# Four-layer graph network on one core: other places for the edge copies, the value loads, the low parts and the flips of layer 0

## What is computed

```python
q = x1.reshape(n, 8, -1).transpose(1, 0, 2) * SCALE      # x1 is x
k = x2.reshape(n, 8, -1).transpose(1, 0, 2)
vv = v.reshape(n, 8, -1).transpose(1, 0, 2)
scores = jnp.einsum('hnd,hmd->hnm', q, k)
scores = jnp.where(adj > 0, scores, NEG_FILL)
attn = jax.nn.softmax(scores, axis=-1)
out = jnp.einsum('hnm,hmd->hnd', attn, vv)
```

## Time and profile before

| | |
|---|---|
| median of 3 runs | 784.59 us (783.59 to 786.24) |
| the profiled execution | 784.18 us, span 782.5 us |
| layer 0 | to about 357.5 us of the span |
| layer 1 | about 357.5 to 588 us |
| layers 2 and 3 | about 588 to 782.5 us |
| busy, share of the span | PE 93%, DVE 84%, ACT 70%, weight loads 58%, POOL 14% |

### The profile page before, as it was taken

How to read it: one execution, slowest core, us unless ns; L and a number is a source line. 1 busy time by engine, 2 the same in 40 slices (tenths; PEclk the granted TensorE clock), 3 DMA queues, 4 the chain that set the end, 5 groups by cost and what they waited for, 6 DMA issues and landing times. The chain is left out here.

```text
span 782.5 us, 22935 instructions
## 1 busy us (share of the span) xinstructions
PE 726.0 (93%) x9908; PEld 454.3 (58%) x9908; DVE 657.7 (84%) x1001; ACT 545.3 (70%) x588; POOL 112.1 (14%) x220
## 2 busy tenths in 40 slices
PE   4798999999999999998889999999966999999996
PEld 1232333333333333336679999999963577776885
DVE  4797999999999999977899999999985757664544
ACT  7898999999999998773699999999904411111000
POOL 1421100310000000004310000000002323321222
PEclk9999999999999999999999999999996999999999
DMA  9998635363545451003271111101005000000001
GB/s 344 247 240 203 173 95 137 89 142 96 136 96 136 98 109 22 2 15 111 53 271 56 57 56 55 41 21 57 3 2 216 1 1 1 2 1 0 28 28 54
DMA packets 42599, 68.39 MB, mean 87 GB/s; under 512 B 4032, under 2 KB 27200, under 8 KB 40832
## 3 DMA queue, kind: packets, MB, share of 16 engines
q1 hardware_dynamic: 32976, 60.08, 25.3%
q0 software_dynamic: 9520, 6.82, 5.2%
HBM read 52.60 MB, written 10.09 MB: 80 GB/s over the span
## 5 line engine op out<-in xcount | busy, mean ns | idle before, releaser
L624 ACT ACTIVATE ex<-scores_ps,joint_shift 128x1024 f32<-128x1024 f32 x256 | 266.7, 1121 | 18.0 <-PE scores_ps L454 17.9
L707 DVE TENSOR_TENSOR esum<-esum,ex 128x1024 f32<-128x1024 f32 x188 | 217.2, 1216 | 1.2 <-ACT ex L624 1.2
L451 PE MATMUL scores_ps<-qst,kst 64*64 64x512 f16 x2048 | 158.7, 385 | 9.0 <-ACT ex L624 9.0
L1480 ACT ACTIVATE steps<-a_all,big_b_head 128x2048 fp8e5<-128x2048 f32 x86 | 163.6, 1988 | 0.0
L1195 PE MATMUL banks<-fx,pos 128*128 128x132 f16 x2048 | 159.4, 221 | 3.9 <-DVE pos L1387 3.7
L470 PE MATMUL mixed_total_ps<-ex,v 128*32 128x512 f32 x1024 | 125.6, 609 | 1.8 <-DMA v<-in_v_dram 1.8
L1195 PEld LDWEIGHTS banks<-fx,pos 128*128 128x128 fp8e5 x2048 | 120.6, 97 | 4.6 <-DVE pos L1387 2.6
L451 PEld LDWEIGHTS scores_ps<-qst,kst 64*64 64x64 f16 x2048 | 48.4, 106 | 116.0 <-ACT ex L624 84.7
L1202 PE MATMUL banks<-fm,edge 128*128 128x66 f16 x2048 | 103.7, 193 | 0.0
L454 PE MATMUL scores_ps<-masks,negI 64*64 64x512 bf16 x1024 | 99.8, 379 | 0.0
L1202 PEld LDWEIGHTS banks<-fm,edge 128*128 128x128 fp8e5 x2048 | 86.1, 97 | 0.0
(11 more groups left out here) (222 smaller groups left out, 722.9 us busy)
## 6 DMA issues: line engine op xcount, KB each, us to landing
adj_raw<-in_adjT_dram SPq DMA_DIRECT2D x32, 512.0 KB, 4.5
qst<-pieces_dram SPq DMA_DIRECT2D x28, 256.0 KB, 5.1
a_all<-score_rows_dram SPq DMA_DIRECT2D x7, 1024.0 KB, 6.6
edge<-masks POOLq DMA_DIRECT2D x32, 128.0 KB, 4.7
edge_copy_dram<-edge SPq DMA_DIRECT2D x1, 4096.0 KB, 17.1
edge_second<-edge_copy_dram SPq DMA_DIRECT2D x1, 4096.0 KB, 12.7
pieces_dram<-high_low SPq DMA_DIRECT2D x14, 256.0 KB, 4.2
ex<-in_x2T_dram SPq DMA_DIRECT2D x2, 1024.0 KB, 8.1
```

Of the source, the lines that this page charges most:

```text
L451: nc.tensor.matmul((one, two)[x][at], keys[rows, x, :], qst[rows, it % 2, half, 2 * p + x, :], start=(half == 0), stop=False, skip_group_c ...
L624: nc.scalar.activation(ex[:, slot(s), 2 * p:2 * p + 2, at], scores_ps[:, u % SR, :].rearrange("p (x n) -> p x n", n=CW), ACT.Exp, bias=joi ...
L707: nc.vector.tensor_tensor(esum[:, heads, at], other, ex[:, slot(s), heads, at], ALU.add).then_inc(summed, 1)
L1480: nc.scalar.activation(steps[:, pair_of(h, k) % SLOTS, jt % GU, :], aall[:, e, :], ACT.Relu, bias=bigh[:, e, jt:jt + 1], scale=BIG, satura ...
```

## The change

Five things move; nothing is computed in another way.

1. **Start.** SP waits for the first load of `v` before it issues `load_x(2)` and `load_x(3)`. DVE makes the low parts of jobs 2 to 4 before the two squares.
2. **Values of group 1** are loaded like those of group 0: once whole rows, then four swapped transfers, in step 4 (after the exponentials of steps 0 to 3), not in step 2.
3. **Edge copies** go by `EDGE_AT`: piece `m` in step `m + 5` or the step after its conversion, if that is later, and each also waits for the exponentials up to that step.
4. **High parts** of jobs 11 to 15 are made in steps 16, 24, 32, 40 and 48, one step earlier; **low parts** stay in step 17 and so on, but ahead of that step's first addition. SP loads and stacks these jobs one step earlier. In each step SP first stores, then loads, then stacks, over all jobs.
5. **Flips**: all 16 behind DVE's last step of layer 0, none in layer 1.

```diff
-    SPLIT_AT = {2: 5, 3: 6, 5: 7, 7: 8, 8: 9, 9: 10, 17: 11, 25: 12, 33: 13, 41: 14, 49: 15}
+    SPLIT_AT = {2: 5, 3: 6, 5: 7, 7: 8, 8: 9, 9: 10, 16: 11, 24: 12, 32: 13, 40: 14, 48: 15}
+    LOW_AT = {s + (s >= 2 * JP): j for s, j in SPLIT_AT.items()}
...
+    EDGE_AT = [max(m + 5, CONVERT_AT.get((m, 1), 0) + 1) for m in range(CONVERTED)]
+    SECOND_V_AT = 4
...
+                sp.wait_ge(v_landed[0], 16)
                 load_x(2)
                 load_x(3)
...
-                    for j in range(3, len(JOBS)):
-                        if LOAD_AT.get(j) == s:
+                    for j in STORE_AT:
+                        if STORE_AT[j] == s:
+                            store_pieces(j)
+                    for j in LOAD_AT:
+                        if LOAD_AT[j] == s:
                             load_natural(j)
-                        if STORE_AT.get(j) == s:
-                            store_pieces(j)
+                    for j in STACK_AT:
                         if STACK_AT[j] == s:
                             stack(j)
...
+                def load_v(g):
+                    pool.dma_start(vt[:, g], tiles(v)[:, :, g * GW:(g + 1) * GW]).then_inc(v_landed[g], 16)
+                    pool.wait_ge(v_landed[g], 16)
                     for h in range(1, HG, 2):
-                        load_swapped(0, h)
...
+                        load_swapped(g, h)
...
+                    if s == SECOND_V_AT:
+                        pool.wait_ge(exp_ready, s * UNITS)
+                        load_v(1)
+                    for m in range(CONVERTED):
+                        if EDGE_AT[m] == s:
+                            if s <= STEPS:
+                                pool.wait_ge(exp_ready, s * UNITS)
+                            keep_edges(m)
...
                 keep_shift(0)
-                make_low(2)
-                square(0)
-                for j in range(3, FIRST):
+                for j in range(2, FIRST):
                     make_low(j)
-                square(1)
+                for i in range(2):
+                    square(i)
...
+                        if i == 0 and s > 2 * JP and s in LOW_AT:
+                            make_low(LOW_AT[s])
...
-                        if i == 1 and s in SPLIT_AT:
-                            make_low(SPLIT_AT[s])
+                        if i == 1 and s < 2 * JP and s in LOW_AT:
+                            make_low(LOW_AT[s])
...
-                        if it in (3, 5, 7) and jp == 0:
-                            flip((it - 3) // 2, i)
+                for c in range(NC):
+                    for part in range(JP // 2):
+                        flip(c, part)
```

More of the change, by code:

```diff
@@ L138, in free_after @@
         return JP * (round_of(c, g) - 1) - 1 if what == "q" and c else -1
-    STORE_AT = {j: STEP_OF[j] + 1 for j in STEP_OF}
+    STORE_AT = {j: s + 1 for s, j in LOW_AT.items()}
     STACK_AT = {j: max(STEP_OF[j], free_after(j)) + 2 for j in STEP_OF}
@@ L350, in load_swapped @@
                         pool.dma_start(vt[to, g, :, at], of_v[of]).then_inc(v_landed[g], 16)
-                def load_first_v():
-                    pool.dma_start(vt[:, 0], tiles(v)[:, :, 0:GW]).then_inc(v_landed[0], 16)
-                    pool.wait_ge(v_landed[0], 16)
+                def load_v(g):
+                    pool.dma_start(vt[:, g], tiles(v)[:, :, g * GW:(g + 1) * GW]).then_inc(v_landed[g], 16)
+                    pool.wait_ge(v_landed[g], 16)
                     for h in range(1, HG, 2):
-                        load_swapped(0, h)
[L358 to L364, removed]
+                        load_swapped(g, h)
                 def keep_edges(m):
@@ L379, in _ @@
                 pool.wait_ge(xs_landed[1], 16)
-                load_first_v()
-                for m in range(AHEAD):
-                    keep_edges(m)
+                load_v(0)
                 for s in range(STEPS + 8):
[L384 to L389, removed]
+                    if s == SECOND_V_AT:
[6 more added lines that the diff above has]
+                            keep_edges(m)
                     if s == RANGE_AT + 2:
@@ L465, in mix @@
                     if s % JP == 0 and it < G:
-                        pe.wait_ge(v_landed[it], 16 * (1 + HG, 3 * HG // 2)[it])
+                        pe.wait_ge(v_landed[it], 16 * (1 + HG))
                     for t in range(2):
@@ L1049, in layer1 @@
             S.sem(n) for n in ("pos_ready", "unit_done", "half_done", "rest_step", "cut", "pieces_joined", "post_step"))
-        left_a, cut_a, negated, counted, fine_made, heads_made, flipped = (
-            S.sem(n) for n in ("left_first_a", "cut_first_a", "negated_first", "fine_counted", "fine_made", "heads_made",
-                               "marks_flipped"))
+        left_a, cut_a, negated, counted, fine_made, heads_made = (
+            S.sem(n) for n in ("left_first_a", "cut_first_a", "negated_first", "fine_counted", "fine_made", "heads_made"))
         a_landed = [S.sem(f"a_landed{e}") for e in range(2)]
@@ L1121, in body @@
                     if h == 0:
-                        sp.wait_ge(flipped, T // TG)
                         sp.dma_start(edge_copy, edge[:]).then_inc(edge_moved, 16)
@@ L1158, in _ @@
                 pe.wait_ge(normed, T - 1)
-                pe.wait_ge(flipped, T // TG)
                 degree.count(pe, ps[:, 1, :], range(T // 2 - 3))
@@ L1238, in largest @@
                                             ).then_inc(most_made, 1)
-                def flip(part):
-                    tt = slice(part * TG, (part + 1) * TG)
-                    marks = edge[:, tt, N - CW:N].bitcast(int32)
-                    nc.vector.tensor_scalar(marks, marks, BITS, BITS, ALU.bitwise_and, ALU.bitwise_xor).then_inc(flipped, 1)
                 nc.vector.memset(wh1[:, :, :, DH:DH + 1], TOP)
@@ L1250, in _ @@
                         measure(t)
-                    if t % TG == 2 and t < T:
-                        flip(t // TG)
                     if t % TG == 0 and t >= 2 * TG:
```

## The result

The changed kernel is slower: 789.32 us median (787.58 to 790.76, 7 runs) against 784.65 us (783.25 to 786.65, 7 runs) of the kernel before beside it, a ratio of 1.0057 (95% interval 1.0042 to 1.0072), so about 4.5 us. That is outside the forecast's range. The profiled execution is the slowest of the seven, 790.76 us with a span of 789.0 us, against 784.18 and 782.5 before.

The account below looks back on a forecast made before the run. Layer 0 was taken as bound by ACT with DMA nearly full to about 72 us, then PE, ACT and DVE, then PE in round 7. Terms +0.6 - 1.4 + 0.1 - 0.3 = -1.0 us gave 783.6 against 784.59, range 780.1 to 787.2.

Parts of the forecast that it names:

- The start: Layer 0 up to unit 3 of step 1: `v` early, adjacency piece 2 late, unit at 34.8 not 30.99, +3.8 us.
- the second halves then land near 24.0: Start: x's second halves, issued after `v` lands near 16.4, land 4.9 + 2.7 us later.
- the 1.8 us added to it for the swapped transfers: Start: q0's DMA time for `v`'s swapped transfers, 2.75 less 0.98 us for an edge copy; piece 2 lands about 27.0.
- the slow start of q0: Start: first packets of `v` of group 0 run about 4.8 us after its issue at 8.40.
- the bound of 28.5: Start: latest landing of piece 2, if a landing follows its last packet by another 1.5 us.
- Steps 2 to 8: Layer 0 after the start: ACT's waits of 1.80, 0.51 and 0.93 us go, -3.24 us, between nothing and -3.24.
- About even: Steps 2 to 8: DMA price of group 1's values as whole rows, 2.7 + 1.8 us against about 4.
- The third rival: Start and steps 2 to 8: DMA backlog not made up before step 6, +5.0 not +0.6 us, 788.0 us; chance 0.10.
- Rounds 2 to 7: Layer 0 round starts: low parts and flips gain, exposed high parts cost 0.52 us each; -1.4 us, between -0.8 and -3.2.
- Rival 2: Rounds: high part stays hidden in ACT's slack ahead of unit 3; rounds -3.2, whole -2.8, 781.8 us; chance 0.14.
- Flips at the end: End of layer 0: 16 flips take 5.4 us in a wait of 5.48 us; +0.1, between 0 and +1.3.
- Layer 1: Layer 1: four flips go, the last ahead of the last tile's statistics; -0.3 us, between 0 and -1.2.

Follow-up runs that it names:

- experiment 6: Changed kernel without SP's wait for `v` in the start and with `v` of group 1 issued in step 2, not 4: 780.07 us, ratio 0.9945.
- experiment 12: Changed kernel, its wait for `v` kept, with `v` of group 1 issued in step 2 instead of step 4: 787.88 us, ratio 1.0031.
- experiment 9: Kernel of experiment 6 with high parts of rounds 2 to 6 moved to the round's second step, behind the third exponential: 782.53 us, ratio 0.9980.
- experiment 8: Kernel before with only the flips at the end of layer 0 and the high and low parts moved: 781.95 us, ratio 0.9971.
- experiment 10: Kernel of experiment 6 with PE making the scores of unit 3 of step 1 ahead of the first mix: 779.30 us, ratio 0.9932.
- Experiment 5: Changed kernel, wait for `v` kept, with adjacency pieces 2 and 3 issued ahead of x's second halves: 789.67 us, ratio 1.0062.
- experiment 11: Changed kernel with SP's wait for `v` between `load_x(2)` and `load_x(3)` instead of ahead of both: 787.06 us, ratio 1.0030.
- experiment 2: Kernel before with only SP's wait for `v` added ahead of `load_x(2)` and `load_x(3)`: 793.58 us, ratio 1.0099.

## Why the prediction was wrong

**The start: the sign was right, the size was not.** The chain was as forecast: `v` early, piece 2 late, unit 3 of step 1 late with it. The wait itself was priced too low, at 3.8 us for 6.58. The step that failed is "the second halves then land near 24.0" and the 1.8 us added to it for the swapped transfers. That took q0's share of the engines for the whole price. Its share was as reckoned (31.3% of the 6 us from 20 to 26, 1.9 us), but q1 also got less done in what it had: the last half was there at 27.02, though `v` had landed 0.8 us earlier than assumed. The forecast also had the slow start of q0 for `v` alone. It came again for the swapped transfers, whose first packets ran 4.6 us and more behind their issue at 15.88, where it had been 2.0 to 2.5 us in the kernel before; nearly all of their 0.52 MB then ran from 20 to 26 us, beside the last half. What they would have cost it had they started sooner, no run shows. Piece 2 was then there at 29.31 instead of 27.0, just above the bound of 28.5, and from there to unit 3 it was 8.26 us, not 7.8.

**Steps 2 to 8: this step failed in kind.** "About even" for the values of group 1 counted the bytes in both shapes, and not when they run. The two waits of 1.80 and 0.93 us went, as forecast, and a new one of 2.68 us came, from values issued 4 us ahead of an adjacency piece. With that one edit put elsewhere the term was right: in experiment 6 the kernel is 1.77 us behind the kernel before at unit 3 of step 1 (32.76) and 1.58 us ahead at `total` of round 2 (111.95 against 113.53), -3.35 us, where -3.24 and +0.26 had been forecast. Which share of it the edge copies have, and which SP's order, no run shows. (The values of group 1 are six transfers in the kernel before, not eight; the bytes are as counted.)

**The third rival** ("the backlog stays", 788.0 us, 10%) came nearest in time: it had +5.0 us up to the rounds, and +5.79 was measured. Its mechanism was half right. The DMA time lost while SP waits is real and is in the 6.58 us. But experiment 12 shows no wait left of it from step 2 on; what stood in step 6 had another cause. The chance was too small, because I held against it only that the edge copies leave the stretch, and not that a megabyte of values moves into it.

**Rounds 2 to 7: right.** `total` of round 7 was to gain 1.4 us on the rounds' start and gained 1.80. By round the forecast had +0.26, -0.40, -0.83, -0.90 and -0.64 at rounds 2 to 6; from 5.79 us behind, the traces have +0.18 (119.50 against 113.53), -0.56 (158.80 against 153.57), -1.03 (198.14 against 193.38), -1.18 (237.44 against 232.83) and -0.99 (276.74 against 271.94). PE's wait for ACT was to be 0.88 us and is 0.86. Rival 2 is out, and experiment 9 shows why the trade is good.

**Flips at the end: right** as to the cover. 16 took 5.45 us, in the wait of 5.48 us of the earlier trace rows, and the first `transpose` follows at once. From `total` of round 7 to it are 37.14 us in the kernel before, and the same in experiments 6, 8 and 10, which have the flips there. The +1.65 us of this stretch come from round 7, and not from the flips: see below.

**Layer 1: not resolved.** The forecast had -0.3 us, the traces have +0.63, with a DMA of `bias` 3.89 us from issue to the instruction that waited for it before (363.11 to 367.00), and 4.86 us after (368.82 to 373.68). From that first `transpose` to `negb` the kernels without flips in layer 1 took between 31.4 and 33.6 us; so the stretch varies by more than the term.

## What to carry to other kernels

A wait ahead of a load prices the whole queue behind it, and lets the DMA engines idle until it ends; before adding one, ask which engine in-order work would have waited anyway, and whether a change in that engine's order (experiment 10) gets the same for nothing. When a transfer is moved or reshaped, look for the next urgent transfer issued within its own landing time in any queue, not only at the bytes. Where a gain could come from either of two engines at a barrier, try the one with the longer path.

## What the runs showed of the hardware that I had not expected

- **The software queue's slow start goes with the second halves.** I read 4.8 us from the issue of `v` to its first packets as a property of the software path. In the changed kernel it is issued at the same time, without the halves in q1, and q0 has packets in the stretch of 10 to 11 us, all of them behind 10.5, so 2.1 to 2.6 us behind the issue:

```profile
q1 hardware_dynamic: 133, 0.24, 68.2%
q0 software_dynamic: 13, 0.05, 54.1%
```

  The same stretch of the kernel before shows q1 alone. `v` landed 7.2 us after its issue instead of 10.8. It is not load as such: the swapped transfers of the kernel before began 2.0 to 2.5 us behind their issue with q1 at a share of 1, in packets of about 1.9 KB (1.28 MB in 679 packets, 19 to 23 us). With the halves in q1, in packets of 8 KB (0.81 MB in 102), it is 4.6 us and more in both kernels: for `v` in the one before, for the swapped transfers in the changed one. Experiment 5, whose swapped transfers are issued at 16.34 with the adjacency pieces ahead of the halves, has their first packets at 18.5 to 19. Whether it is the size of the packets or something else about the halves was not tested. The 1 us that the Trainium skill gives for it ("DMA: Bandwidth & Descriptors", Specifications), weighed in the prediction, is nearer to the shorter of the two than my reading was, though it isn't reached here either.

- **Round 7 has two lengths.** From its `total` to the first `transpose` of the end it is 37.14 us in six of the fourteen traces, those of the kernel before and of experiments 5, 6, 8, 10 and 11. It is 38.7 to 39.9 us in the other eight, the changed kernel's among them. PE has idled 2.45 to 3.25 us ahead of it in all. In the 15 us around this `total` the granted clock is 1.00 in the six short ones, 0.89 in seven of the long ones and 0.77 in experiment 2; two rows of busy time, of the changed kernel and of the kernel before:

```profile
310.00:325.00 15.00, 12.55 (x152) 3.94 (x144) 12.14 (x12) 9.32 (x10) 0.00 (x0) 0.89 0.01 2
```

```profile
305.00:320.00 15.00, 11.74 (x168) 4.15 (x160) 14.66 (x18) 10.18 (x11) 0.00 (x0) 1.00 0.01 2
```

  The profiled pair differs by 6.6 us and the medians by 4.7; this is 1.65 us of the first. What decides it was not tested: it falls on either side at nearly the same idle time, so one profile for each kernel can't price an edit there to better than 1.65 us.
